# A longer experts' tail, and a new order of mixing, norms, rotations and values around it

## The reference

```python
x = x + attention0(layernorm(x), ctx)   # quantised self and cross attention
x = x + moe(layernorm(x))               # 32 experts of width 96, all computed, mixed by routing weights
x = x + attention1(layernorm(x), ctx, itok)
x = x + ffn1(x_norm)                    # gated, width 704, x_norm = layernorm(x)

# moe, per expert:   y += (silu(x @ wg.T) * (x @ wu.T)) @ wd.T * cw[:, None]
# attention1:
q_c = q @ W_dq                          # compressed to 96
q_nope, q_rope = q_c @ W_uq, rope(q_c @ W_qr)
scores = (q_nope . k_nope + q_rope . k_rope) * scale, masked by segment
out = (softmax(scores) @ v) @ W_o
```

## Time and profile before

| | us |
|---|---|
| median of 3 runs | 842.53 (841.06 to 845.69) |
| the profiled execution | 842.54 |
| its span, first to last instruction | 840.7 |

### The profile page before, as it was taken

How to read it: one execution, slowest core, us unless ns; L and a number is a source line. 1 busy time by engine, 2 the same in 40 slices (tenths; PEclk the granted TensorE clock), 3 DMA queues, 4 the chain that set the end, 5 groups by cost and what they waited for, 6 DMA issues and landing times.

```text
span 840.7 us, 14354 instructions
## 1 busy us (share of the span) xinstructions
PE 785.3 (93%) x4848; PEld 669.3 (80%) x4848; DVE 663.6 (79%) x1567; ACT 535.7 (64%) x1236; POOL 464.2 (55%) x782
## 2 busy tenths in 40 slices
PE   3687999999999999999899999999999999898997
PEld 3466788888888888888788878898888867577787
DVE  7789999899998989989889794865754678977634
ACT  6788877787778877788774555433332268974432
POOL 3688969779586895858855576433310004980000
PEclk9799999999999999999999999999999999899999
DMA  7000120011200121000200323968423000100001
GB/s 242 14 0 1 39 76 1 2 39 39 76 1 1 39 61 54 2 2 1 68 26 14 127 65 89 241 166 267 133 65 88 1 1 14 51 14 1 1 1 51
DMA packets 28265, 45.60 MB, mean 54 GB/s; under 512 B 3936, under 2 KB 18080, under 8 KB 28064
## 3 DMA queue, kind: packets, MB, share of 16 engines
q1 hardware_dynamic: 26800, 41.31, 16.7%
q10 hardware_dynamic: 1392, 3.37, 1.1%
HBM read 43.49 MB, written 1.18 MB: 53 GB/s over the span
## 4 chain that ended last, share of the span: by engine, by line
PE 59%; DVE 21%; ACT 11%; issue 4%; DMA 2%; POOL 1%; SPq 1%; ACTq 0%; DVEq 0%
PE PS L789 17%; PE PS L859 8%; PE PS L649 6%; PE PS L744 4%; PE PS L718 3%; PE PS L680 3%; PE PS L969 2%; DVE st L1664 2%; PE PS L701 2%; PE PS L690 2%; PE PS L671 2%; DVE yb L1566 2%; ACT P L1127 2%; DVE cat L1570 1%; DMA l_KM<-share 1%
## 5 line engine op out<-in xcount | busy, mean ns | idle before, releaser
L2272 POOL TENSOR_SCALAR raw<-raw,mvq,rsq 128x128 f32<-128x128 f32 x312 | 183.4, 602 | 1.6
L789 PE MATMUL PS<-xq,WH 128*128 128x512 f32 x472 | 148.4, 396 | 0.0
L789 PEld LDWEIGHTS PS<-xq,WH 128*128 128x128 f32 x472 | 86.3, 190 | 17.2 <-issue 1.1
L649 PE MATMUL PS<-WH,xq 128*128 128x256 f32 (+1 forms) x256 | 89.5, 368 | 7.0 <-DVE xq L1570 7.0
L789 PE MATMUL PS<-xq,WL 128*128 128x512 f32 x236 | 92.4, 392 | 0.0
L649 PE MATMUL PS<-WL,xq 128*128 128x256 f32 (+1 forms) x256 | 85.4, 352 | 0.0
L1127 ACT ACTIVATE P<-PS,sm 128x256 f32<-128x256 f32 x128 | 61.0, 497 | 25.9 <-DVE sm L1728 25.8
L859 PE MATMUL PS<-xq,m_hh 128*128 128x256 f32 x384 | 69.9, 282 | 3.1 <-ACT m_hh L1013 2.4
L1664 DVE BATCH_NORM_STATS2 st<-raw 128x6 f32<-128x128 f32 x320 | 70.5, 276 | 1.8 <-ACT raw L1099 1.8
L718 PE MATMUL PS<-PT,vr 128*128 128x256 f32 x256 | 66.4, 382 | 3.8 <-ACT PT L1013 3.8
L680 PE MATMUL PS<-kT,qT 128*128 128x256 f32 x256 | 65.9, 380 | 1.8 <-ACT qT L1116 1.8
(11 more groups left out here) (302 smaller groups left out, 2175.3 us busy)
## 6 DMA issues: line engine op xcount, KB each, us to landing
wst<-in_wgu SPq DMA_DIRECT2D x24, 256.0 KB, 3.7
l_KM<-share SPq DMA_DIRECT2D x16, 384.0 KB, 4.0
wst<-in_wall SPq DMA_DIRECT2D x18, 256.0 KB, 3.1
l_KM<-share SPq DMA_DIRECT2D x16, 256.0 KB, 5.1
dst<-in_wdn SPq DMA_DIRECT2D x24, 128.0 KB, 3.2
wst<-in_wkvx SPq DMA_DIRECT2D x8, 256.0 KB, 3.2
l_KM<-share SPq DMA_DIRECT2D x16, 128.0 KB, 4.5
m_pre<-in_wo ACTq DMA_DIRECT2D x1, 2048.0 KB, 8.7
```

Source lines behind the costliest of these rows:

```text
L649: t = e.matmul(PS[:, b, o:o + n], xq[s][:, k, c * 128:(c + 1) * 128], W[:, k, w0:w0 + n], start=(k == 0 and i == 0), stop=(k == 1 and i == 1))
L789: t = e.matmul(PS[:, b, :], W[wi][:, gu, k, :], a[:, k, cols], start=(n == 0), stop=(n == 5))
L2272: t = e.tensor_scalar(v, v, mvq[:, par, n, 0:1], rsq[:, par, n:n + 1], ALU.add, ALU.mult)
```

## The change

- `MOE`: the pieces whose halves are kept apart are now six (18 to 23) instead of four. The last two pieces' share copies get buffers of their own: `CB` has six, the two new ones in `S[1]` and `S[2]`.
- PE: the four `outmix` stand behind the products of items 42 to 45 instead of behind the last ones; `turn` 0 and 1 stand behind the gate and up products of item 46, `compress` 0 and 1 behind those of item 47, and the two parts of `queries(0)` ahead of the last two `down`. The four `keymix` come last. ACT's copies move with them.
- DVE: `settle(0)` runs in steps of nine between the items; behind the experts come the rotations of block 0 and only then `settle(1)`. Each of the other rotation parts stands one c later than before, and ahead of `scale`.
- Buffers: the cosine and sine products of pieces 0 to 2 no longer use `S`, all pieces share two pairs of buffers; `CT` has a second set in those buffers.
- POOL: `add_q` waits until both pieces of a part have their sine product, then sums both; all `load_f` come behind the last sum.
- ACT: one-element activations (`touch`) with Exp and Silu stand ahead of the first real ones. `values(2)` goes from n = 8 to n = 7, behind `turn_p(5)`.

The order of PE and the banks:

```diff
-MOE = [(j, h) for j in range(20) for h in range(2)] + [(j, h) for h in range(2) for j in range(20, 24)]
+TAIL = 18
+MOE = [(j, h) for j in range(TAIL) for h in range(2)] + [(j, h) for h in range(2) for j in range(TAIL, 24)]
...
     for n in range(2, len(MOE)):
         if MOE[n][0] >= NPRE:
             do("gate_up", *MOE[n])
+        if n == 46:
+            do("turn", 0)
+            do("turn", 1)
+        if n == 47:
+            do("compress", 0)
+            do("compress", 1)
         do("down", *MOE[n - 2])
+        if 41 < n < 46:
+            do("outmix", n - 42)
+    do("queries", 0, 0)
     do("down", *MOE[-2])
-    do("outmix", 0)
-    do("outmix", 1)
+    do("queries", 0, 1)
     do("down", *MOE[-1])
-    do("outmix", 2)
-    do("turn", 0)
-    do("turn", 1)
-    do("outmix", 3)
-    do("compress", 0)
-    do("compress", 1)
     do("keymix", 0)
-    do("queries", 0, 0)
     do("keymix", 1)
-    do("queries", 0, 1)
     do("keymix", 2)
     do("keymix", 3)
...
-QUERIES = {1: (4,), 2: (5,), 3: (6,), 4: (7,)}
-FPIECES = ((0,), (1, 2), (3, 4), (5,), (6, 7, 8))
+QUERIES = {1: (3,), 2: (4,), 3: (5,), 4: (6,), 5: (7,)}
...
     do("queries", 1, 0)
-    do("turn", 2)
-    do("turn", 3)
     for n in range(12):
-        if n % 2 == 0 and n > 3:
+        if n in (4, 6):
             do("values", (n - 4) // 2)
         if n < 8:
             do("scores", n)
-        if n == 0:
-            do("queries", 1, 1)
+        if n == 1:
+            do("turn", 2)
+            do("turn", 3)
+        for m in QUERIES.get(n, ()):
+            do("queries", m // 2, m % 2)
+        if n == 1:
             do("compress", 2)
             do("compress", 3)
         if 1 < n < 9:
             do("turn_p", n - 2)
-        for m in QUERIES.get(n, ()):
-            do("queries", m // 2, m % 2)
+        if n == 7:
+            do("values", 2)
+        if n == 10:
+            do("values", 3)
...
-            "lp": lambda c, z: 2 * (c < 6) + z, "lv": lambda bb, z: 2 + z,
+            "lp": lambda c, z: (2, 4)[c == 6] + z, "lv": lambda bb, z: (2 + z) if bb != 2 else (2, 3, 0, 1)[z],
...
 # ACT, behind the experts
+            swap_q(0, 0)
+            swap_q(0, 1)
+            e.activation(touch[:], idf[:, 0:1], ACT.Exp)
             take_km(0)
...
+                if n == 9:
+                    e.activation(touch[:], idf[:, 0:1], ACT.Silu)
...
 # DVE
-                    for _ in range(7):
+                    for _ in range(9):
                         next(settling, None)
...
-            weave(settling)
-            weave(settle(1))
             turn_q(0, 0)
             turn_q(0, 1)
-            turn_q(1, 0)
+            weave(settle(1))
...
                 if n < 8:
                     soft(n)
+                if n == 0:
+                    turn_q(1, 0)
+                for m in QUERIES.get(n, ()):
+                    turn_q(m // 2, m % 2)
                 if n == 8:
                     add_l(1)
                 if 0 < n < 9:
                     scale(n - 1)
-                if n == 0:
-                    turn_q(1, 1)
-                for m in QUERIES.get(n, ()):
-                    turn_q(m // 2, m % 2)
...
 # POOL
+                w.wait_ge(turned_q.sem, turned_q.at[bb, 2 * part + 1])
+                w.emptied(("qr", bb, 2 * part + 1))
                 for u in range(2 * part, 2 * part + 2):
                     n = 4 * bb + u
-                    w.wait_ge(turned_q.sem, turned_q.at[bb, u])
-                    w.emptied(("qr", bb, u))
...
-            for part in range(2, 4):
+            for part in range(2, 8):
                 add_q(part // 2, part % 2)
             w.wait_ge(downed.sem, downed.at[MOE[-1]])
-            for n in range(5):
-                for m in QUERIES.get(n, ()):
-                    add_q(m // 2, m % 2)
-                for j in FPIECES[n]:
-                    load_f(j)
+            for j in range(9):
+                load_f(j)
```

More of the change, by code:

```diff
@@ L410, in program @@
             sb("l_pad", [128, 336], F32, c2)
-            CT = x2T[:].rearrange("p k (a t) -> p (k a) t", t=256)
+            CT = [x2T[:].rearrange("p k (a t) -> p (k a) t", t=256)[:, 2 * z:2 * z + 2, :] for z in range(4)]
+            CT = [CT, [prea[:, i, :].rearrange("p (a t) -> p a t", a=2) for i in (8, 9, 12, 13)]]
             fsg = [sb(f"f_sg{i}", [128, 512], F32, c2) for i in range(3)]
@@ L417, in program @@
             S = [S0] + [sb(f"l_S{i}", [128, 1024], F32, c2) for i in (1, 2)]
-            tqc = [S[2 - n][:, 0:512] for n in range(3)] + [prea[:, 8 + n % 2, :] for n in range(3, 16)]
-            tqs = [S[2 - n][:, 512:1024] for n in range(3)] + [prea[:, 12 + n % 2, :] for n in range(3, 16)]
+            tqc, tqs = ([prea[:, o + n % 2, :] for n in range(16)] for o in (8, 12))
+            CB = [KM[:, z, :, :].rearrange("p a b -> p (a b)") for z in range(4)] + [S[z][:] for z in (1, 2)]
         flat = lambda t: t[:].rearrange("p a b -> p (a b)")
@@ L555, in program @@
         gate_in, share_out = sem("gate_in"), sem("share_out")
-        share_in = [sem(f"share_in{z}") for z in range(4)]
+        share_in = [sem(f"share_in{z}") for z in range(6)]
         wo_in, fsc_in, seg_in, stored = sem("wo_in"), sem("fsc_in"), sem("seg_in"), sem("stored")
@@ L926, in scores2 @@
                 w.wait_ge(keys_in, 4)
-                for z in range(8):
-                    emptied(("km", z))
                 for z in range(2):
+                    for y in range(4 * z, 4 * z + 4):
+                        emptied(("km", y))
                     b = fill(("ls", c, z))
@@ L1361, in scalar, with take_lt, take_qc, take_bp @@
                         copy(cwT[:, z * 512:(z + 1) * 512], PS[0:32, b, :]).then_inc(free[b], 1)
+            def take_lt(bb):
+                b = w.filled(("lt", bb))
+                copy(x2T[:, :, bb * 256:(bb + 1) * 256], PS[:, b, :].rearrange("p (k t) -> p k t", k=2)).then_inc(free[b], 1)
+            def take_qc(bb):
+                b = w.filled(("qc", bb))
+                copy(qcT[:, bb * 256:(bb + 1) * 256], PS[0:96, b, 0:256]).then_inc(free[b], 1)
+            def take_bp(z):
+                b = w.filled(("bp", z))
+                copy(Bp[:, 2 * z:2 * z + 2, :].rearrange("p a b -> p (a b)"), PS[:, b, :]).then_inc(free[b], 1)
             for n, (j, h) in enumerate(MOE):
@@ L1383, in scalar @@
                     take_aw(3)
-            split_h(len(MOE) - 1)
[L1385 to L1391, removed]
+                if 41 < n < 46:
+                    take_bp(n - 42)
+                if n == 46:
+                    take_lt(0)
+                    take_lt(1)
+                if n == 47:
+                    take_qc(0)
+                    take_qc(1)
+            split_h(len(MOE) - 1)
             def exps2(c):
@@ L1410, in take_lv @@
                 w.filled(("qc", 3))
-                if bb:
-                    w.filled(("lo", bb - 1))
+                if bb > 1:
+                    w.filled(("lo", bb - 2))
+                if bb == 1:
+                    w.wait_ge(*summed(3, 3))
                 for z in range(4):
                     b = w.filled(("lv", bb, z))
-                    copy(CT[:, 2 * z:2 * z + 2, :].rearrange("p a b -> p (a b)"), PS[:, b, :]).then_inc(free[b], 1)
+                    copy(CT[bb % 2][z], PS[:, b, :].rearrange("p (a t) -> p a t", a=2)).then_inc(free[b], 1)
             def split_f(bb):
@@ L2503, in stage_share @@
             def stage_share(j):
-                if j > 3:
-                    w.wait_ge(weighed.sem, weighed.at[j - 4, 1])
+                if j > 5:
+                    w.wait_ge(weighed.sem, weighed.at[j - 6, 1])
                 first = 128 * j // 96
@@ L2509, in stage_share @@
                     n = rows.stop - rows.start
-                    e.dma_start(CB[j % 4][rows, :], share[expert:expert + 1, :].to_broadcast([n, 1024])).then_inc(share_in[j % 4], 16)
+                    e.dma_start(CB[j % 6][rows, :], share[expert:expert + 1, :].to_broadcast([n, 1024])).then_inc(share_in[j % 6], 16)
             for z in range(2):
```

50 lines of the change are left out of this document (18 added, 32 removed).

## The result

The changed kernel takes 860.8 us (median of 4 runs, 856.6 to 861.3) against 843.7 (841.1 to 845.7): **1.0192 times the kernel before, 95% interval 1.0168 to 1.0216**. The profiled execution took 861.06 us with a span of 859.1. Slower was forecast, but 851.0, and the range ended at 854.5.

A forecast was written before the change was run, and what follows sets the result against it. DVE was taken to bound the kernel from the second half's norm to `project(0)`, PE behind it. 842.5 + 4.4 (up to `project(0)`) + 0.6 (behind it) + 3.5 (clock) = 851.0 us, chance 0.45; range 842.0 to 854.5.

The forecast's parts named there:

- The bound: From the second half's norm to `project(0)` the path is DVE's; behind that it is PE's, to the end.
- Before the first rotation: New PE order: last gate and up products end at 677.3, DVE's first rotation starts at 683.2, 3.9 us earlier.
- The tail's 3.1 us: Second half's norm now stands behind block 0's four rotated pieces: both done at 697.9 instead of 694.8.
- DVE's path: Up to `project(0)`: 3.1 us later, a sixth soft step 2.5, waits 1.2 less: 4.4 us later.
- the waits: DVE's waits ahead of `project(0)`: 5.0 us (3.5 for scaling products meeting sums, 1.5 for ACT) instead of 6.2.
- the four met products: Four DVE scaling products meet POOL's two sums ahead of `project(0)`: 0.9 us each, 3.5 charged.
- the sixth soft step: Last rotation part stands one round later, so one more `soft` comes ahead of it on DVE: +2.5 us.
- Behind the first projection, values: The 2.44 us wait ahead of `project(2)` goes, three new waits of 3 us come: net +0.6 us.
- I take one such loss: Low clock after PE's 3.4 us stall ahead of `project(0)`: one loss of 3.5 us counted, earlier stalls none.
- at nothing: Costs put at zero: six tail pieces, Exp's table, and `load_f` on POOL from about 746 to 790 at the latest.
- The rule of the Trainium skill: A DVE instruction with two SBUF inputs contends with a GpSimd instruction reading SBUF; a reduction never does.

The follow-up runs named there:

- order_hold: Changed kernel with the old order of queries, rotations, scaling and turned probabilities, and POOL's weights' pieces 5 to 8 held behind the first norm: 850.4 us (1.0085).
- both_old_order: `order_hold` on the old tail, leaving of the change only paired sums, held weights' pieces and the values: 845.4 us (1.0027).
- norm_first: `order_hold` with the second half's norm ahead of block 0's rotations, and a PE order to suit: 853.8 us (1.0107).
- turn_late_h1: `order_hold` with the second half's turnings moved behind the first score and block 1's last rotated piece: 850.3 us (1.0083).
- v_only: Kernel before with only the second set for the values' output and the third values product a step earlier: 843.4 us against 844.3 (0.9991).
- two_holds: `both_old_order` with weights' pieces 5 and 6 held for the first norm behind the projection, 7 and 8 for the second: 842.1 us against 842.8 (0.998).
- fill2: Changed kernel with 2, 2, 3 and 4 products whose result is overwritten put into PE's four longest stalls: 854.8 us (1.0106).
- fill_holds: Changed kernel with filling products (2, 2, 3) in the three stalls up to the first projection, and two holds of the weights' pieces: 849.4 us (1.0058).
- after_holds: Changed kernel with only POOL's weights' pieces 5 and 6 held for the first norm behind the projection, 7 and 8 for the second: 853.3 us (1.0105).
- hold_f: Changed kernel with POOL's weights' pieces 5 to 8 held until the first norm behind the projection is through: 856.3 us (1.0132).

## Why the prediction was right or wrong

**The bound** was read rightly for the changed kernel: its first projection waits 3.22 us for DVE's last cosine. In the kernel before, and in the versions with the old order, PE gets there without waiting, so there the two are level, and that the path up to `project(0)` is DVE's alone was not shown.

**Before the first rotation**: the last gate and up product ends at 676.4 (forecast 677.3), the first cosine is at 681.8 (683.2), the second norm ends at 696.4 (697.9), each 0.9 to 1.5 us early.

**The tail's 3.1 us**: because of that, norm and first pieces end only 1.8 us later than before, from the mark. In the old order of rotations the tail does cost 3.4 us at the first projection (154.3 in `order_hold` against 150.9 in `both_old_order`), but by another way: 2.2 us from the end of norm and pieces, and 1.2 from longer waits of DVE (5.1 us against 3.9), since PE's turnings of the second half wait for that norm and DVE then waits for PE. The prediction had no such wait, so it is luck that its size is near. This is read from two profiles; the two runs that were to isolate it, `norm_first` and `turn_late_h1`, brought other waits in its place.

**DVE's path**: forecast 4.4 us up to the first projection, measured 3.8 with the clock kept up. That they are so near is in part luck: the tail gave 1.8 where 3.1 was forecast, and the waits were 5.6 us where 5.0 were: 4.0 in the four met products (1.01 each against 0.9) and 1.5 for ACT. With the sixth soft step, 2.5, that is 1.8 + 2.5 + 5.6 - 6.2 = 3.7.

**Behind the first projection, values**: forecast +0.6 with three new waits, and these came; the projections span 45.7 us in `v_only` and 46.1 in `two_holds` against 44.8: +0.9 to +1.3 in single executions. In the time of all executions of `v_only` no difference shows.

**Clock: the first failed step.** "I take one such loss" of 3.5 us, in the first projection; there it came, with 2.5. What failed is that the stalls ahead of it were put at nothing, as lying beside DVE's path: they cost 4.3 us in the changed kernel's profiled execution (1.5 to 2.9 in two others with the same code up to there), 6.8 with the projection. By the medians, filling the stalls gave 6.0 us (`fill2`), and 3.9 on top of the two holds (`fill_holds`). From the kernel before I took that a fall beside DVE's path costs little. There the soft steps behind the fall had their scores in time; after the change the next scores and the next rotated piece stand behind PE's stall, and DVE waits for them (1.65 + 0.99 us at 732).

**Weights' pieces: the second, "at nothing".** The prediction asked only whether the pieces are done in time for the FFN. It had them run from 746 to 790 and did not ask what DVE does there: the sixth scaling product and the norm, several of whose small steps, like that product, have two inputs in SBUF. They cost 6.7 us in the profiled execution, and holding them gave 7.5 by the medians (`after_holds`). The rule of the Trainium skill that was cited for the sums covers these meetings too.

With the measured terms the sum is 842.5 + 3.8 + 4.3 + 2.5 + 1.3 + 6.7 = 861.1, and the profiled execution took 861.06. That is no proof: each term is a difference of the starts in the table, so they add up to its 8.1 + 10.5 us whatever the causes. What bears the account out is `fill_holds`, which takes away the two causes, but for one fall of the clock in its profile, and leaves 4.9 us of the 16.

## What to carry to other kernels

When work of POOL is moved into one block, look at every DVE operation in the stretch where it now runs, the smallest most of all: steps of 0.16 us can each cost nearly a whole POOL operation, as three of the nine in one chain did here. A stall of one engine that was free because another had its inputs already is not free once the next inputs stand behind it; follow what the stalled engine does next, and who waits for that. A wait that is removed at one edge (the values) is worth only what the next latest edge leaves.

## What the hardware showed that was not expected

The same stall at the same place is followed by a fall of the clock in one execution and not in another: behind 2.32 us ahead of the third score the next eight products took 2.07 us in the changed kernel, and 1.16 behind 2.33 us in `hold_f` (timeline, PE):

```profile
711.44 1.16 PE L941 MATMUL PS<-l_KZ,m_pre 128*128 128x128 f32 x8 [2.33 <-POOL m_pre L2411]
```

In `fill_holds` the clock fell behind stalls of 1.30 and 0.83 us, and in `fill2`, with 1.29 and 0.83 at the same place, it did not (timelines of the two, PE, the values products there):

```profile
765.38 3.57 PE L973 MATMUL PS<-l_PT,l_BDK 64*64 64x512 f32 x16 [0.83 <-ACT l_PT L1032]
```

```profile
765.43 1.95 PE L975 MATMUL PS<-l_PT,l_BDK 64*64 64x512 f32 x16 [0.83 <-ACT l_PT L1034]
```

The changed kernel's own four runs spread with the clock, from 856.6 us at a mean of 0.985 to 861.3 at 0.975. And a DVE step that meets a POOL operation does not slow in proportion to its size: 0.16 us became 1.13, about the length of the POOL operation (1.27).
